# A block-transposed expert loop with three weight buffers, rows stored by SyncE, and gate scaling split between GpSimd and ScalarE

## What is computed

```python
gate = jax.nn.sigmoid(topk_vals)                  # one expert of 8 for each token
xs = x[:, None, :] * gate[:, :, None]
def body(acc, inp):
    wg, wd, e = inp                               # wg 256 x 1024, wd 512 x 256
    h = _silu_mul(xs @ wg)                        # silu(g) * u
    return (acc + jnp.where(ids_flat == e, h @ wd, 0), None)
```

## Time and profile before

| | |
|---|---|
| device time, median of 3 runs | 128.91 us |
| device time of the profiled execution | 129.24 us |
| span of the profiled execution | 127.6 us |
| TensorE products busy | 122.1 us (96%) |
| TensorE weight loads busy | 106.1 us (83%) |
| VectorE busy | 79.4 us (62%) |
| ScalarE busy | 53.4 us (42%) |
| GpSimd busy | 35.4 us (28%) |
| granted TensorE clock | 1.0 throughout |
| moved by DMA | 25.02 MB, mean 196 GB/s |

### The profile page before, as it was taken

One profiled execution on the slowest core, in us unless ns is written; L12 is line 12 of the kernel. 1 busy time (PEld: TensorE's weight loads), 2 busy tenths in 40 slices (PEclk: granted clock), 3 DMA queues, 4 the chain that ended last, 5 costly groups with the idle time before them and its releaser, 6 DMA issues.

```text
span 127.6 us, 2426 instructions
## 1 busy us (share of the span) xinstructions
PE 122.1 (96%) x822; PEld 106.1 (83%) x822; DVE 79.4 (62%) x175; ACT 53.4 (42%) x113; POOL 35.4 (28%) x65
## 2 busy tenths in 40 slices
PE   4989999999999999999999999999999999999990
PEld 1248776788888857999999999999999978999990
DVE  0799695997899999875575553505040428922471
ACT  1678796829987546322222222242221337200000
POOL 7804040003879300040303030303030301687500
PEclk9999999999999999999999999999999999999999
DMA  3784999999993210129797989888982031033437
GB/s 83 207 281 37 330 360 244 181 207 397 385 380 136 82 51 0 46 81 318 264 321 258 295 275 277 307 280 303 281 303 63 9 86 51 13 89 104 112 101 244
DMA packets 15748, 25.02 MB, mean 196 GB/s; under 512 B 1296, under 2 KB 12632, under 8 KB 15736
## 3 DMA queue, kind: packets, MB, share of 16 engines
q1 hardware_dynamic: 13368, 20.66, 53.1%
q0 software_dynamic: 1456, 3.41, 8.2%
q10 hardware_dynamic: 912, 0.80, 1.9%
HBM read 18.78 MB, written 6.08 MB: 195 GB/s over the span
## 4 chain that ended last, share of the span: by engine, by line
PE 80%; POOL 6%; issue 5%; DMA 4%; DVE 2%; ACT 0%; DVEq 0%; POOLq 0%
PE ps L1112 25%; PE ps L1126 13%; PE ps L300 6%; POOL q_sb L458 6%; PE ps L302 5%; PE ps L301 5%; PE ps L975 5%; PE ps L988 4%; PE ps L981 4%; PE ps L1066 4%; DMA q_sb<-sorted_rows,slot_row 2%; PE ps L1053 2%; DMA sorted_rows<-yrow 2%; PE ps L1060 2%; DVE x_sb L895 1%
## 5 line engine op out<-in xcount | busy, mean ns | idle before, releaser
L1112 PE MATMUL ps<-xgT,gu 128*128 128x144 f32 x256 | 34.2, 287 | 0.0
L1112 PEld LDWEIGHTS ps<-xgT,gu 128*128 128x128 f32 x256 | 32.3, 190 | 0.5 <-issue 0.2
L826 DVE TENSOR_TENSOR wqkv<-rz,ps 128x288 f32<-128x288 f32 x16 | 7.3, 454 | 25.5 <-ACT rz L576 25.5
L440 POOL DMA_DIRECT2D sorted_rows<-yrow x9 | 5.0, 558 | 54.7 <-DVE yrow L821 54.7
L1126 PE MATMUL ps<-wqkv,dn 128*128 128x144 f32 x128 | 17.4, 289 | 0.0
L576 ACT ACTIVATE rz<-ps 128x288 f32<-128x288 f32 x16 | 6.5, 409 | 25.0 <-PE ps L1112 25.0
L1126 PEld LDWEIGHTS ps<-wqkv,dn 128*128 128x128 f32 x128 | 16.1, 190 | 0.0
L432 POOL DMA_INDIRECT sorted_rows<-xn,slot_row x8 | 9.8, 1220 | 15.4 <-ACT xn L514 13.6
L300 PE MATMUL ps<-xT_hi,sgu_hi 128*128 128x512 f32 x32 | 13.0, 407 | 0.0
L301 PE MATMUL ps<-xT_lo,sgu_hi 128*128 128x512 f32 x32 | 12.6, 394 | 0.0
L302 PE MATMUL ps<-xT_hi,sgu_lo 128*128 128x512 f32 x32 | 12.6, 394 | 0.0
(11 more groups left out here) (162 smaller groups left out, 231.3 us busy)
## 6 DMA issues: line engine op xcount, KB each, us to landing
gu<-in_L_ffn_w_gate_up_dram SPq DMA_DIRECT2D x8, 1024.0 KB
dn<-in_L_ffn_w_down_dram SPq DMA_DIRECT2D x8, 512.0 KB
sorted_rows<-zeros SPq DMA_DIRECT2D x1, 2592.0 KB, 18.0
wqkv<-sorted_rows SPq DMA_DIRECT2D x10, 144.0 KB
sorted_rows<-yrow POOLq DMA_DIRECT2D x9, 128.0 KB, 2.1
sgu<-_ffn_shared_gate_up_dram SPq DMA_DIRECT2D x1, 1024.0 KB, 6.2
wqkv<-in_L_attn_w_qkv_dram SPq DMA_DIRECT2D x3, 256.0 KB, 3.7
x_sb<-in_L_attn_x_dram SPq DMA_DIRECT2D x2, 256.0 KB, 3.6
```

Of the source, the lines that this page charges most:

```text
L826: V.tensor_tensor(hr[:, 2 * h:2 * h + 2, :].rearrange("p f s -> p (f s)"), act_sb[:, h, 0:2 * SLOTS], ps[:, 2 * h + 1, 0:2 * SLOTS], ALU.m ...
L1112: ins = mm(ps[:, 2 * h + u, (f % 2) * SLOTS:(f % 2 + 1) * SLOTS], gu[p][:, kc, col:col + P], xgT[:, kc, :], start=(kc == 0), stop=(kc == K ...
```

## The change

- **Transposes.** TensorE transposes nothing in the loop any more. Rows are loaded into `xg` in four transfers of 32 partitions each, in pieces of 64 floats, so that one block transpose (32x32 blocks) on VectorE gives `xgT` (`sorted_in`). The output goes from the two PSUM banks to `yrow` by one block transpose (`rows_out`) and is stored in four transfers of the same form (`row_store`). Both cover 160 rows (`NSQ` = 5 blocks of `SQ` = 32) instead of 144. The order of columns that comes out of it (even and odd ones apart) is met by the weights: `w_gate_up` is loaded with two neighbouring rows in each partition, and the down products read every second column of `dn`.
- **Parts.** Gate/up goes in three parts (8, 4 and 4 products) with banks (0,1), (2,3), (4,7), and silu, product and semaphores follow.
- **Weights.** A third buffer pair, laid over `xT_raw` and `ez`; expert 2 is loaded before the loop, expert e + 3 after expert e.
- **Queues.** SP stores the rows of the previous tile, then loads the rows of the tile after next, then refills. In the tail SP stores two quarters of the last tile and ScalarE's queue two. GpSimd has only scatter and gather left.
- **Gate scaling.** GpSimd scales token tiles 0 to 2 itself, ScalarE tiles 3 to 7 after q/k/v tile 11.
- **VectorE's order.** `kv_scan(0)` and `(1)` move from the shared tiles behind expert tile 0, `(2)` and `(3)` behind tile 1; the other attention work moves by one or two tiles.

```diff
-        xgT = sb("xgT", [P, KC, SLOTS], F32)
-        yT = sb("yT", [P, KC * SLOTS], F32)
-        yrow = sb("yrow", [P, 2, D], F32)
-        yrest = sb("yrest", [KC * REST, 2, P], F32)
+        xgT = sb("xgT", [P, KC, NSQ * SQ], F32)
+        yrow = sb("yrow", [P, NSQ, SQ * KC], F32)
+        gu_of = [gu[0][:, :, :], gu[1][:, :, :], xT_raw[:, :, :]]
...
-        gu_dram = w_gate_up.rearrange("e (c p) n -> e p c n", p=P)
+        gu_dram = w_gate_up.rearrange("e (p c) n -> e p c n", c=KC)
+        PARTS = ((0, 1), (2,), (3,))
+        def row_store(eng, t, q, s_store):
+            rows = sorted_rows[bass.ds(t * SLOTS, NSQ * SQ), q * SQ * KC:(q + 1) * SQ * KC]
+            eng.dma_start(rows.rearrange("(j p) f -> p j f", p=SQ), yrow[q * SQ:(q + 1) * SQ, :, :]).then_inc(s_store, 16)
...
-                    sp.wait_ge(s_xgT, t + 2)
-                    sorted_load(t + 2)
+                    sp.wait_ge(s_yrow, t + 1)
+                    for q in range(P // SQ):
+                        row_store(sp, t, q, s_ystore)
+                    sp.wait_ge(s_xgc, t + 2)
+                    sorted_load(t * SLOTS + 3 * SLOTS, s_xg)
...
-                sp.dma_start(gu[p][:, :, :], gu_dram[e + 2]).then_inc(s_gu[p], 16)
+                sp.dma_start(gu_of[p][:, :, :], gu_dram[e + 3]).then_inc(s_gu[p], 16)
...
+            sorted_load(SLOTS, s_xg0)
+            sp.wait_ge(s_lrow, 1)
+            sp.wait_ge(s_q, 2 * NH)
+            expert_load(2)
...
-            sp.wait_ge(s_xg, 16 * ends[7] + 16)
-            sp.wait_ge(s_lastrest, 1)
+            sp.wait_ge(s_xg, 64 * ends[7] + 64)
+            sp.wait_ge(s_lastrow, 1)
+            for q in range(2):
+                row_store(sp, ends[7], q, s_ylast_sp)
...
+            for i in range(POOL_SCALED):
+                pool.tensor_scalar(xn[:, i, :], xn[:, i, :], gate[:, i:i + 1], None, ALU.mult).then_inc(s_xsp, 1)
             pool.wait_ge(s_zero, 16)
...
-                    if t in (8, 9):
-                        scale_tokens({8: range(0, 3), 9: range(3, NT)}[t])
+                    if t == 11:
+                        scale_tokens(range(POOL_SCALED, NT))
...
+            def sorted_in():
+                V.transpose(xgT[:, :, :], xg.rearrange("p j (f c) -> p c j f", c=KC)).then_inc(s_xgc, 1)
+            def rows_out(t, s_done):
+                dve.wait_ge(s_down, t)
+                dve.wait_ge(s_ystore, 64 * t)
+                V.transpose(yrow[:, :, :].rearrange("p j (f c) -> p c j f", c=KC), ps[:, 5:7, 0:NSQ * SQ]).then_inc(s_done, 1)
+            def expert_tile(t, first=False):
+                if not first:
+                    rows_out(t, s_yrow)
+                expert_part(t, 0)
+                expert_part(t, 1)
+                dve.wait_ge(s_xg, 64 * t + 64)
+                dve.wait_ge(s_gup, 3 * t + 3)
+                sorted_in()
+                expert_part(t, 2)
...
-                        if h == 0:
-                            pe.wait_ge(s_yrow, t + 1)
-                            transpose_back(t + 1)
-                    transpose_sorted(4, s_xg, 16 * t + 16)
+                    pe.wait_ge(s_yrow, t + 1)
-                                ins = mm(ps[:, 5 + c, 0:SLOTS], dn[p][:, f, c * P:(c + 1) * P], hr[:, f, :],
+                                ins = mm(ps[:, 5 + c, 0:SLOTS], dn_of[p][:, f, :].rearrange("p (m c) -> p c m", c=KC)[:, c, :], hr[:, f, :],
```

More of the change, by code:

```diff
@@ L190, in build @@
         s_sdn = sem("s_sdn")
-        s_gu = [sem(f"s_gu{p}") for p in range(2)]
-        s_dn = [sem(f"s_dn{p}") for p in range(2)]
+        s_gu = [sem(f"s_gu{p}") for p in range(3)]
+        s_dn = [sem(f"s_dn{p}") for p in range(3)]
         s_zero = sem("s_zero")
@@ L218, in build @@
         s_xs = sem("s_xs")
+        s_xsp = sem("s_xsp")
         s_scatter = sem("s_scatter")
@@ L266, in build @@
         s_down = sem("s_down")
-        s_yT = sem("s_yT")
-        s_yback = sem("s_yback")
         s_yrow = sem("s_yrow")
[L270 to L273, removed]
+        s_ystore = sem("s_ystore")
+        s_lastrow = sem("s_lastrow")
+        s_ylast_sp = sem("s_ylast_sp")
+        s_ylast_act = sem("s_ylast_act")
         s_gather = [sem(f"s_gather{i}") for i in range(NT)]
@@ L597, in attention_hi @@
                 A(att_hi[:, c, cols], kvsum[:, c, cols], ACT.Copy).then_inc(s_atth, 1)
+            act.wait_ge(s_lastrow, 1)
+            for q in range(2, P // SQ):
+                row_store(act, total, q, s_ylast_act)
             attention_hi(0)
@@ L869, in _ @@
             V.tensor_tensor(wout_lo, wout[:, :, :], wout_hi.bitcast(F32), ALU.subtract).then_inc(s_plo, 1)
-            first_tile(4)
+            expert_tile(4)
             head_reciprocals(3)
-            first_tile(5)
+            for c in range(KC):
+                dve.wait_ge(s_kvs, 2 * NH)
+                V.tensor_tensor(kvsum[:, c, :], q_sb[:, c, :], kvsum[:, c, :], ALU.mult).then_inc(s_qkv_sum, 1)
+            expert_tile(5)
             dve.wait_ge(s_rhigh, 1)
             V.scalar_tensor_tensor(rden_split, rden, low_row[:, 0:1], rden_hi.bitcast(F32), ALU.mult, ALU.add).then_inc(s_rsplit, 1)
-            first_tile(6)
+            expert_tile(6)
             with dve.Fori(E - 1, total) as t:
-                expert_tile(t, 1, 32 * t - 32 * (E // 2))
+                expert_tile(t)
+            rows_out(total, s_lastrow)
             attention(0)
-            rows_copy(total, 0, 32 * (E // 2), LAST_BACK)
             attention(1)
@@ L1100, in _ @@
             for e in range(E):
-                p = e % 2
-                pe.wait_ge(s_gu[p], 16 * (e // 2) + 16)
+                p = e % 3
+                pe.wait_ge(s_gu[p], 16 * (e // 3) + 16)
                 with pe.Fori(ends[e - 1] if e else 0, ends[e]) as t:
                     pe.wait_ge(s_xgc, t + 1)
-                    for h in range(2):
-                        if e == 0 and h == 1:
+                    for h in range(3):
+                        if e == 0 and h == 2:
                             pe.wait_ge(s_denc, 1)
+                            pe.wait_ge(s_sh, LAST)
@@ L1108, in _ @@
                         for u in range(2):
-                            for f in (2 * h, 2 * h + 1):
+                            for j, f in enumerate(PARTS[h]):
                                 for kc in range(KC):
                                     col = u * F + f * P
-                                    ins = mm(ps[:, 2 * h + u, (f % 2) * SLOTS:(f % 2 + 1) * SLOTS],
-                                             gu[p][:, kc, col:col + P], xgT[:, kc, :], start=(kc == 0), stop=(kc == KC - 1))
+                                    ins = mm(ps[:, (GATE, UP)[u][h], j * SLOTS:(j + 1) * SLOTS],
+                                             gu_of[p][:, kc, col:col + P], xgT[:, kc, 0:SLOTS], start=(kc == 0), stop=(kc == KC - 1))
```

176 lines of the change are left out of this document (65 added, 111 removed).

## The result

| | before | after |
|---|---|---|
| median of 18 runs, us | 129.14 (128.76 to 131.13) | 127.56 (126.07 to 130.11) |
| ratio to before | | 0.9835 [0.9807, 0.9863] |
| span of the profiled execution, us | 127.6 | 125.8 |
| eight expert tiles, us | 52.44 | 50.87 |
| from the last down product to the end of the span, us | 24.3 | 24.5 |

The kernel became faster, by 1.65% or 2.1 us. The ratio leaves out executions more than 1.5% above the fastest of their kernel (6 of the 18 after the change); without them the medians are 129.0 and 127.1 us, and it is medians of this kind that stand in the table of the experiments. The prediction said 124.0 us, 5.2 us less; the median of all runs lies just outside its range, by 0.06 us. What shows the mistake is the loop: it was to take 47.8 us and takes 50.87. The runs after the change also spread over 4 us, those of before over 2.4.

The account below looks back on a forecast made before the run. TensorE's weight loads bound the tile, DMA next; afterwards the gather chain and TensorE end together. Loop 47.5 + 0.3 us and the tail gave span 122.3, 5.3 less, rounded to 5.2: 129.24 - 5.2 = 124.0 us, range 122.8 to 127.5.

Parts of the forecast that it names:

- TensorE -5.5 us: Whole TensorE side: transposes and holes leave, -4.9 us in eight tiles (5.94 us each), the rest before and after the loop.
- Strided weight loads, 0 extra: Down products reading every second weight column: taken as 0 extra, upper bound 16.1 us; slower loads kept as a 0.06 chance.
- Block transposes 0.5 us: Two 128x320 transposes per tile on VectorE: 0.5 us each, upper bound 2.4, cost on the path 0.
- 256 B packets 17 ns: Row loads and stores, 1280 packets a tile: 17 ns each, 1.4 us a tile; upper bound 48 ns, 3.8 us.
- rival 1: Row packets bind the expert tiles, row loads waiting behind refills: 126.5 us, or 132.5 with all at 48 ns; chance 0.18.
- One follows the down product at once: Output transpose on VectorE in each tile: starts right after the down product, nearly 4 us before TensorE needs the banks.
- Landing 2.1 us: Row stores and loads on SyncE's queue: each lands 2.1 us after issue, as a 128 KB store does.
- Loop waits: Eight expert tiles: DMA keeps pace with little to spare, so 0.3 us was added for waits.
- SyncE, ten issues in 4.5 us: SyncE in each tile: four stores, four loads, two refills at about 0.45 us each, 4.5 of 5.94 us.
- GpSimd's scaling, 0.65 us each: Start: three token tiles scaled on GpSimd at 0.65 us, at worst 1.29; scatters 1.4 us earlier, hidden by the shared tiles.
- The tail: After the loop: gathers start 5.5 us after the last down product; dense adds end 119.7, span ends 122.3 us.
- rival 3: Gather chain sets the end, last stores or 256 B landings 1 to 2 us late: 125 to 126 us; chance 0.12.

Follow-up runs that it names:

- pitch_two: Changed kernel with two row buffers, tiles 160 rows apart and SyncE's tile loop unrolled with constants (one tile per expert); 123.97 us, ratio 0.952.
- no_refill: Changed kernel without the five refills of expert weights (experts 3 to 7 use the weights of 0 to 2); 123.0 us, ratio 0.948.
- static_rows: Changed kernel with SyncE's tile loop unrolled to constant trip counts, making row addresses constants; one row buffer, tiles 144 rows apart; 125.71 us, ratio 0.973.
- act_store: Changed kernel with the four row stores of each tile issued on ScalarE's queue, ahead of its first silu; 132.18 us, ratio 1.020.

## Why the prediction was wrong

- **TensorE -5.5 us: right.** The undisturbed tile takes 5.88 us (said 5.94); without refills the loop is 47.1 us (said 47.5). It is what the change can give, and the changed kernel doesn't collect it.
- **Strided weight loads, 0 extra: right.** The down product's loads take 196 ns on average against 190, but it runs its 16 in 1.96 us where nothing holds it. By the Trainium skill ("SBUF — State Buffer", Door 1) no extra was due; the trace agrees on the path, and shows 6 ns a load beside it.
- **Block transposes 0.5 us: right**, 515 ns for 128x320 from PSUM, 505 from SBUF.
- **256 B packets 17 ns: too low.** The line through the earlier trace rows gives 18, and in a stretch of the tail (104.9 to 107.1 us) 352 packets on SyncE's queue come to about 24 ns each, well under the bound of 48. That makes 1.9 us a tile for 1280 packets instead of 1.4, and 6.1 us of work instead of 5.6, a little over the 5.94 of the tile. The DMA share reaches 0.96 to 0.99 in three tiles, so rival 1 was close to its edge, but the two longest tiles have less. What is left of rival 1 shows with two buffers: the loop of `pitch_two` is 1.2 us above that of `no_refill`, and its one large hole waits for a row load behind refills. The Trainium skill ("DMA: Bandwidth & Descriptors", Specifications) says that below 512 B the engines do read-modify-write. The prediction took that as pointing toward 48 ns; the trace shows half of it, and rows stored in 256 B pieces land in 1.6 us when alone.
- **"One follows the down product at once": this step failed.** In the loop `rows_out` came 1.5 to 4.0 us behind the end of the down product; in six of seven cases it waited for a store (the first, 1.5, came behind two scans). The prediction gave `yrow` no reuse: it asked whether TensorE's banks would be free in time, and never whether the buffer was. Its own numbers would have raised the question: transpose 0.5, SyncE's four issues 1.8, landing 2.1 make 4.4 us of 5.94, with 1.5 to spare only at an idle landing. The nearly 4 us until TensorE needs the banks again were the wrong slack too, since the product for the down product stands behind `rows_out` in VectorE's order: the trace shows 2.7.
- **Landing 2.1 us: mis-sized.** The earlier trace rows takes it from stores of the kernel before, and in the tail it holds (1.57). Behind a refill it is 3.4 to 5.1 us in the changed kernel. The prediction saw that "a row load waits behind the refills ahead of it" (rival 1), but priced it as throughput, (work - 5.94) a tile, not as latency in a round trip. Loop waits were put at 0.3 us and are 3.4 (50.87 - 47.5).
- **SyncE, ten issues in 4.5 us: right as a sum** (0.53 and 0.42 each), but not harmless: four of them lie in the round trip, and what SyncE does with registers around them costs 1.4 us of the kernel's time (127.10 against 125.71) and 1.7 of the loop, as `static_rows` shows.
- **GpSimd's scaling, 0.65 us each: 1.1 us**, within the bounds; the first scatter went at 31.01 us, not 1.4 us earlier than 30.90, and the loop still started at 50.46, as said.
- **The tail**: gathers at D + 6.5 instead of D + 5.5 (D is the end of the last down product), since the unused load, which SyncE waits for, went out behind late stores and landed at D + 3.4 instead of D + 2.0. The cause is the round trip again. From D to the end of the span 24.5 us (said 23.9). This is rival 3 in small, 0.6 us.

Together: 3.4 - 0.3 = 3.1 us in the loop and 0.6 in the tail are 3.7, less 0.14 us by which the loop started sooner (50.46 against 50.6): 3.6. The span of the profiled execution is 125.8 us instead of 122.3, a difference of 3.5.

## What to carry to other kernels

A buffer that is filled, stored and filled again has a period of its own: write, issues, landing, next write. A wait in it costs nothing until the slack of the engine that waits is used up (2.7 us here), and from there on it costs its full amount. Reckon it for every single buffer of a loop and compare it with the new tile, not the old one, whenever a change shortens the tile. Take the landing from rows with the loop's own traffic ahead of it, not from an idle stretch. Here constant addresses took 1.7 us off the loop, a second buffer on top of them 0.7 more, and another queue added 5.5. And before traffic is moved away from one waiter, look at who stands behind it in the new place.

## What the hardware showed that I had not expected

- A 40 KB store of 256 B pieces lands 1.6 us after its issue when alone and 3.2 to 5.9 behind a 1.5 MB refill with one row buffer. Another queue doesn't help (4.6 median on ScalarE's).
- Register addresses cost SyncE 0.17 us ahead of the first store of a group and up to 0.1 us for each, and reading a loop bound and entering the loop up to 0.8 us more where it stood in the way; through the round trip that was 1.4 us of 127.1.
- Three of four holes of 2.1 to 2.9 us on TensorE were followed by a stretch at a lower granted clock (0.70 over 5.75 us in one), which cost 1.1 to 1.7 us more; holes of up to 1.3 us, one in each of seven tiles of `act_store` (granted clock 1.00 throughout), were not.
